# Row sums and value halves of an attention kernel, moved from VectorE and ScalarE to DMAs and TensorE

## The reference

```python
h = group_norm1(x, n1_g, n1_b)
f = dwconv(h, w3, b3) + dwconv(h, w5, b5) + dwconv(h, w7, b7)
g = sigmoid(conv1x1(f, gate_w, gate_b))
x = x + conv1x1(f * g, proj_w, proj_b)
h = group_norm1(x, n2_g, n2_b)
q, k, v = conv1x1(h, ...)             # N = 9216 pixels, 64 channels each
attn = softmax(q^T k / 8, axis=-1)    # 9216 x 9216 for each image
out = x + (attn v)^T
```

## Time and profile before

| | us |
|---|---|
| Median of 3 runs (3044.29 to 3048.2) | 3047.66 |
| The profiled execution, its own time | 3046.7 |
| Its span, first to last instruction | 3045.0 |
| TensorE busy | 2736.0 (90%) |
| GpSimd busy | 2311.9 (76%) |
| ScalarE busy | 2218.4 (73%) |
| VectorE busy | 1967.6 (65%) |
| DMAs of GpSimd's queue: 320.90 MB | 51.8% of 16 engines |

### The profile page before, as it was taken

One profiled execution on the slowest core, in us unless ns is written; L12 is line 12 of the kernel. 1 busy time (PEld: TensorE's weight loads), 2 busy tenths in 40 slices (PEclk: granted clock), 3 DMA queues, 4 the chain that ended last, 5 costly groups with the idle time before them and its releaser, 6 DMA issues.

```text
span 3045.0 us, 87180 instructions
## 1 busy us (share of the span) xinstructions
PE 2736.0 (90%) x36568; PEld 1138.5 (37%) x36568; DVE 1967.6 (65%) x2081; ACT 2218.4 (73%) x2288; POOL 2311.9 (76%) x2056
## 2 busy tenths in 40 slices
PE   7898999998989898999988989999999999999998
PEld 4343333333333333333333333333333333333333
DVE  4766666666666666666657666666666666666665
ACT  4577777777777777777767777777777777777777
POOL 1467777777778787877865878787888888887886
PEclk9999999999999999999999999999999999999999
DMA  6148666666666666666601656666666666666561
GB/s 195 35 102 182 130 131 128 129 126 129 132 127 131 128 131 127 131 133 126 122 7 41 130 125 135 132 129 130 130 135 134 134 135 134 134 135 128 124 128 21
DMA packets 124020, 371.20 MB, mean 122 GB/s; under 512 B 17640, under 2 KB 43752, under 8 KB 123120
## 3 DMA queue, kind: packets, MB, share of 16 engines
q0 software_dynamic: 88128, 320.90, 51.8%
q1 hardware_dynamic: 35504, 44.75, 5.5%
HBM read 16.41 MB, written 9.44 MB: 8 GB/s over the span
## 4 chain that ended last, share of the span: by engine, by line
PE 36%; POOL 21%; issue 13%; DVE 11%; DMA 11%; ACT 6%; POOLq 0%; ACTq 0%; SPq 0%; DVEq 0%
POOL arena L486 17%; PE ps L1060 16%; PE ps L1049 12%; DMA accD<-arena 11%; DVE mxp L827 6%; PE ps L1069 5%; ACT arena L576 3%; POOL accD L501 2%; DVE arena L853 2%; POOL mseed L519 2%; ACT ps L617 2%; PE ps L1182 2%; DVE accD L850 1%; ACT pvx L591 1%; DVE pvc L874 1%
## 5 line engine op out<-in xcount | busy, mean ns | idle before, releaser
L827 DVE TENSOR_REDUCE mxp<-ps 128x1 f32<-128x1024 f32 x1296 | 1581.0, 1224 | 775.2 <-PE ps L1069 774.1
L486 POOL TENSOR_TENSOR arena<-arena 128x512 f32<-128x512 f32 x1224 | 1703.2, 1391 | 417.7 <-ACT arena L576 351.9
L576 ACT ACTIVATE arena<-ps,bnd 128x1024 f32<-128x1024 f32 x1296 | 1382.0, 1110 | 502.3 <-PE ps L1049 483.8
L1060 PE MATMUL ps<-arena,vals 64*64 64x512 f32 x10368 | 1294.6, 613 | 0.2 <-DVE pvc L874 0.2
L1049 PE MATMUL ps<-arena 64*64 64x512 f16 x15552 | 1087.0, 382 | 145.1 <-ACT ps L617 140.1
L617 ACT ACTIVATE ps<-mseed 128x1024 f32<-128x1024 f32 x612 | 628.8, 1027 | 176.6 <-POOL mseed L519 125.5
L1049 PEld LDWEIGHTS ps<-arena 64*64 64x64 f16 x15552 | 463.1, 108 | 589.8 <-issue 322.1
L1069 PE MATMUL ps<-arena,QM 64*64 64x512 f16 x5184 | 528.5, 395 | 121.8 <-DVE mxp L827 116.9
L501 POOL DMA_DIRECT2D accD<-arena x544 | 494.4, 910 | 94.2 <-DMA accD<-arena 56.4
L1060 PEld LDWEIGHTS ps<-arena,vals 64*64 64x64 f32 x10368 | 385.0, 137 | 419.9 <-issue 333.7
L1069 PEld LDWEIGHTS ps<-arena,QM 64*64 64x64 f16 x5184 | 153.5, 105 | 664.1 <-DVE mxp L827 574.3
(11 more groups left out here) (124 smaller groups left out, 807.1 us busy)
## 6 DMA issues: line engine op xcount, KB each, us to landing
accD<-arena POOLq DMA_DIRECT2D x612, 512.0 KB, 5.1
arena<-arena SPq DMA_DIRECT2D x144, 64.0 KB, 3.5
arena<-in_x_rows SPq DMA_DIRECT2D x8, 816.0 KB, 9.7
xs<-in_x SPq DMA_DIRECT2D x4, 1152.0 KB, 15.5
f_scratch<-arena SPq DMA_DIRECT2D x32, 144.0 KB
f<-f_scratch SPq DMA_DIRECT2D x16, 288.0 KB, 9.7
QM<-arena SPq DMA_DIRECT2D x72, 64.0 KB, 3.5
xst<-arena SPq DMA_DIRECT2D x72, 64.0 KB, 4.4
```

The costliest lines, as they stand in the source:

```text
L486: nc.gpsimd.tensor_tensor(accA[:, n % 2, :], accA[:, n % 2, :], e, ALU.add).then_inc(adda_free, 1)
L576: nc.scalar.activation(E[:, :, slot_of(n % 2, p), :], ps[:, S_BANK + 2 * buf:S_BANK + 2 * buf + 2, :], ACT.Exp, scale=bnd[:, 6:7]).then_in ...
L827: nc.vector.reduce_max(flat(mxp[:])[:, v:v + 1], flat(ps[:, bank:bank + 2, :]), AX.X).then_inc(mx_free, 1)
L1060: a = nc.tensor.matmul(ps[C * t:C * t + C, ACC_BANK + r, :], V[rows, p, t, :], E[rows, t, slot_of(par, p), :], start=(p == 0), stop=(p == ...
```

## The change

It alters five things at once.

- **Fills from the fp16 row.** `fill_source`, `mseed` and its semaphore go. `seed` reads the fp16 row in `QS` itself, waits for `m_ready`, and ScalarE does the scaling in the same instruction.
- **Dumps at an even pace.** `accD` has a second copy for alternate blocks, so the first dump of a block is issued after pair 1 and then one after every odd pair, 18 in all as before.
- **Folds as DMAs.** `sum_dumps` on VectorE goes, and so does `total` on GpSimd but for an image's last block. In the next block GpSimd issues three accumulating DMAs: after pair 5 one that adds the one half of `accD` to the other (512 KB), after pairs 8 and 11 one each that adds 512 columns of it to `accA` (256 KB), each waiting for the one before. TensorE sums `accA` directly, after pair 18 and not 12.
- **Value halves by TensorE.** `turn_pv` and `sum_pv` go. `twice` is a 128 x 64 matrix with two identities; `value_sums` multiplies `pvc` by it right behind the row sums, two matmuls of 256 columns into the same PSUM bank. ScalarE copies 512 columns instead of 256 to `fin`.
- **Order on the engines.** VectorE does `add_pv` behind the first `reduce_max` of a block and not ahead of it; the reciprocals follow after the visits of pairs 17 to 24, one each, and before only after odd ones; the multiplication on GpSimd is after pair 31, not 33. Between the images the same steps move by a few chunks.

```diff
-ROW_SUMS = 12
+ROW_SUMS = 18
-DUMP_AFTER = (8, 9, 11, 12, 14, 15, 17, 18, 20, 21, 23, 25, 27, 29, 31, 33, 35, 35)
-DUMPS_SUMMED = 6
+NDUMP = NPAIR // 2
+FOLD_AFTER = (5, 8, 11)
...
+            def fold_dumps(b, j, i):
+
+                n, d = blk(b, j), dumped_block(b, j)
+                if i == 0:
+                    for k in (0, 1):
+                        pool.wait_ge(dumped[k], dumps_before(b, j + 1, 0))
+                    pool.dma_start(accD[:, d % 2, 0, :], accD[:, d % 2, 1, :], accum_op=ALU.add).then_inc(folded, 16)
+                else:
+                    pool.wait_ge(folded, folds_before(d, i))
+                    pool.wait_ge(adda_free, NSLOT + NPAIR * (n + 1))
+                    pool.dma_start(accA[:, n % 2, :], accD[:, d % 2, 0, (i - 1) * CH:i * CH], accum_op=ALU.add
+                                   ).then_inc(folded, 16)
...
             def attend(b, j):
                 n = blk(b, j)
-                fill_source(n)
                 first_a(n)
...
+                for p in range(1, NPAIR):
+                    if p > 1:
+                        add_a(n, p)
+                    if j < LASTS and p % 2:
+                        dump(b, j, p // 2)
+                    if j and p in FOLD_AFTER:
+                        fold_dumps(b, j - 1, FOLD_AFTER.index(p))
+                    if j and p == 31:
+                        normalize(n - 1)
...
-                act.wait_ge(mseed_ready, n + 1)
+                act.wait_ge(m_ready, n + 1)
                 act.wait_ge(e_ready, NPAIR * n + p)
-                nc.scalar.activation(ps[:, S_BANK + 2:S_BANK + 4, :], mseed[:, n % 2, :].unsqueeze(1).to_broadcast([P, 2, CH]), ACT.Copy
-                                     ).then_inc(seeded, 1)
+                nc.scalar.activation(ps[:, S_BANK + 2:S_BANK + 4, :], QS[:, n % 2, 2, :].unsqueeze(1).to_broadcast([P, 2, CH]), ACT.Copy,
+                                     scale=ONE * C).then_inc(seeded, 1)
...
+            def value_sums(n, bank):
+                pe.wait_ge(acc_free, n + 1)
+                for h in (0, 1):
+                    a = nc.tensor.matmul(ps[C * h:C * h + C, bank, HCH:CH], twice[:], pvc[:, h, :], start=True, stop=True)
                 a.then_inc(rs_ready, 1)
 
-            def row_sums(n, bank):
-                pe.wait_ge(sum_ready, n + 1)
+            def row_sums(b, j, bank):
+                n = blk(b, j)
+                if j < LASTS:
+                    pe.wait_ge(folded, folds_before(dumped_block(b, j) + 1, 0))
+                    sums = accA[:, n % 2, :]
+                else:
+                    pe.wait_ge(sum_ready, b + 1)
+                    sums = accS[:]
```

More of the change, by code:

```diff
@@ L555, in _ @@
                 if b + 1 < B:
-                    total(blk(b, NBLK - 1))
+                    total(b)
         @block.scalar
@@ L583, in move_pv @@
                 if n:
-                    act.wait_ge(pv_summed, 2 * n)
+                    act.wait_ge(rs_ready, n)
                 nc.scalar.activation(flat(pvc[:]), ps[:, ACC_BANK, :], ACT.Copy).then_inc(acc_copied, 1)
[L587 to L591, removed]
             def copy_row_sums(n, bank):
@@ L675, in _ @@
                         move_pv(blk(b, 0) - 1)
-                    if b and c == 4:
-                        turn_pv(blk(b, 0) - 1)
-                    if b and c == 3:
+                    if b and c == 6:
                         copy_row_sums(blk(b, 0) - 1, MX_BANK + 1)
@@ L843, in add_b, with sums_out @@
                     nc.vector.tensor_tensor(ps[:, SUM_BANK, :], ps[:, SUM_BANK, :], e, ALU.add).then_inc(addb_free, 1)
[L845 to L855, removed]
+            def sums_out(b):
                 dve.wait_ge(addb_free, NPAIR * (b + 1))
-                if n:
-                    dve.wait_ge(sum_ready, n)
+                if b:
+                    dve.wait_ge(sum_ready, b)
                 nc.vector.tensor_copy(accB[:], ps[:, SUM_BANK, :]).then_inc(accb_out, 1)
-                dve.wait_ge(accb_out, n + 1)
+                dve.wait_ge(accb_out, b + 1)
             def reciprocals(n, k):
@@ L911, in attend @@
                         reduce_max(NVIS * (n + 2) + v, v)
+                    if j and p == 0:
+                        add_pv(n - 1)
                     if j == LASTS and p + 1 < NPAIR:
                         add_b(b, n, p + 1)
[L914 to L917, removed]
                     if j == 0 and p < NPAIR - AHEAD and p % 8 == 7:
@@ L932, in _ @@
             row_masks()
+            nc.vector.tensor_tensor(twice[:], ident[:, 0:C], ident[:, C:P], ALU.add).then_inc(twice_ready, 1)
             row_stats(0)
@@ L963, in _ @@
                         add_pv(blk(b, 0) - 1)
-                    if b and c in (4, 5):
-                        for k in range(RECS // 2 * (c - 4), RECS // 2 * (c - 3)):
+                    if b and c in (6, 7):
+                        for k in range(RECS // 2 * (c - 6), RECS // 2 * (c - 5)):
                             reciprocals(blk(b, 0) - 1, k)
-                    if b and c == 6:
-                        sum_pv(blk(b, 0) - 1)
+                    if b and c == 8:
                         normalize(blk(b, 0) - 1)
-                    if b and c == 7:
-                        write_out(b - 1, NBLK - 1)
                 x1_stats(NCH - 1)
+                if b:
+                    write_out(b - 1, NBLK - 1)
                 dve.wait_ge(bn_done, NCH * (b + 1))
@@ L1013, in _ @@
             add_pv(n)
-            sum_pv(n)
             dve.wait_ge(rs_ready, n + 1)
@@ L1198, in _ @@
             pe.wait_ge(conv_out, BESIDE)
+            pe.wait_ge(twice_ready, 1)
             pe.wait_ge(mat_in, 32)
```

114 lines of the change are left out of this document (53 added, 61 removed).

## The result

The changed kernel takes 2754.76 us (median of 4 runs, 2749.4 to 2756.6) against 3047.93 us before: ratio 0.9035, 95% interval 0.9019 to 0.9052. The profiled execution took 2755.12 us, 291.6 us less than the one before.

The account below looks back on a forecast made before the run. TensorE was taken as the bound mid-block, late GpSimd fills at the edge. 78.5 - 7.7 (gaps) - 2.4 (clock) + 1.1 (added) = 69.5 us a block; 288 us less over 32 blocks plus 12 gave 2747 us, range 2690 to 2840.

Parts of the forecast that it names:

- Step 1 and 2, fills and clock: At the block's edge on TensorE: the 4.03 us gap for fills goes, and 2.4 us of low clock with it.
- Step 3, add_pv: At the block's edge: the 0.79 us gap for a maximum goes, but weigh waits 0.5 us for add_pv.
- Step 4, sum_dumps: On TensorE: the 1.82 us gap a block for a maximum behind sum_dumps' two additions on VectorE goes.
- turn_pv and sum_pv: On TensorE: gaps of 0.77 and 0.27 us a block go when these two steps leave ScalarE and VectorE.
- Step 5, value sums: On TensorE behind the row sums: two fp32 matmuls add 0.6 us a block to the path.
- A block: The period of one block falls from 78.5 to 69.5 us, for 32 blocks 288 us less.
- GpSimd: GpSimd's block: 65.0 us of work, 1.4 fold wait, 1.0 dump waits, together 67.4 us, 2 us under TensorE.
- The last blocks: The last block of each image has the same edge without dumps or maxima: 6.1 us less each, twice is 12.
- the fold's wait: On GpSimd: the fold after pair 8 waits for its DMA by 1 to 2 us.
- B: Rival: GpSimd and its DMAs become the bound, 72.0 us a block, 2827 us in all; chance 0.19.
- C: Rival: the edge keeps a 2.5 us gap and the clock falls, 73.9 us a block, 2896 us; chance 0.08.
- D: Rival: slower, GpSimd stands while each fold lands; at 14 us a fold, 3160 us; chance 0.03.

Follow-up runs that it names:

- the fills alone: Kernel before the change, with only ScalarE's fills taken from the fp16 row and fill_source gone: 2855.95 us, ratio 0.9363 against the kernel before.

## Why the prediction came out as it did

Forecast 2747, measured 2754.76 us. By its steps:

- **Step 1 and 2, fills and clock**: 4.03 + 2.4 us an edge. The mechanism is shown by the fills alone: 194 / 34 = 5.7 us an edge, of which 3.2 are waits and 2.6 clock. The wait was read from one edge longer than the average; the prediction's check, that the waits of the trace make 7.6 us a block and the edge shown 7.68, holds for the sum only, since that edge has more of the waits for fills (4.80 us for 140.1 / 34 = 4.1) and less of those for maxima (2.88 for 3.4). What the prediction did not see is that the dumps' pace works on the same gap: with the pace changed, the old fills would have cost 32 us and not 200. The sum came out right because it counted the gap once.
- **Step 3, add_pv**: 0.5 us forecast, taken between two bounds, and 0.52 + 0.19 = 0.71 in the edge shown, for another cause: that these are near each other is luck. The wait for add_pv is 0.19 us, 6.6 in all for the 17 that the prediction named as a sign; the 0.52 is a `write_out` of 1.59 us where one that lies alone takes 0.47, and with GpSimd held back it goes. The prediction had no term for an instruction that takes longer beside another engine's.
- **Step 4, sum_dumps**: forecast 1.82 us a block, 51 / 34 = 1.5 measured. **turn_pv and sum_pv**: 0.77 + 0.27 forecast, less 0.6 for the matmuls, so 0.4 net; measured from the changed kernel's side 74 / 34 = 2.2. As a measure of that the term was mis-sized, in sum_pv: in the changed kernel GpSimd is adding just when VectorE adds the halves, which take 1154 ns each in the mean for 615 in the kernel before. What undoing this part costs is thus not what the change gained by it; the gain against the kernel before was not measured by itself.
- **Step 5, value sums**: 0.6 forecast, 0.53 measured.
- **A block**: 69.5 forecast, 69.56 measured. The agreement to 0.1 us is partly luck: the waits for fills gave less than forecast, the clock more, and the mean holds one block of 83.7 us that nobody forecast.
- **GpSimd**: its sum of 67.4 us left 2 us; the slack was 3.9. The fold in whole landed after 7.1 us, as worked out, and GpSimd waited 47.3 / 34 = 1.4 us for landed folds (7.5 of the 47.3 once, beside the loads). What was too high is mostly the work: GpSimd is busy for 62.98 us in the window of a block, for 65.0 forecast, though the earlier trace rows had 63.26 and the prediction itself says that the work stays the same. The waits at the head of a block are 0.35 us in the edge shown, for 1.0. All first folds, issue to landing, and all accumulating dumps:

```profile
DMA to landing us min/median/max: 4.5/7.1/23.1
```

```profile
DMA to landing us min/median/max: 4.4/5.0/20.9
```

- **The last blocks** were put at 12 us. The 32 blocks gave 286.0 of a forecast 288, all the rest together 5.6 of 12: this term carries most of the miss of 8 us. It was taken from one edge, 6.1 us for each image. The traces show 2.6 us less from the last block of the first image to the second block of the other (217.16 us for 219.71 between GpSimd's first adds) and 4.1 less from the second image's last block to the end (68.61 for 72.73), and 0.8 us more before block 1. What holds the time there was not tested.
- **Signs.** The clock over the edges (1.00), the waits for fills (7.3 us, under 20), the block and the fold's wait came as named. Two did not: the waits for maxima are 32.5 us and not under 30, because of `write_out`, and those for add_pv 6.6 and not 17.
- **Rivals.** B fell: ScalarE waited 10.6 us in all for dumps, and 5.2 us of added work cost 1.3. C fell: no gap over 1.2 us at a usual edge. D fell: the slowest first fold of all other blocks took 8.7 us; beside the loads one took 23.1, and there TensorE did wait for it, once.

By an estimate from the figures of the Trainium skill, DMA: Bandwidth & Descriptors (Anatomy of one DMA), which the prediction weighed, a DMA of 512 KB would take 3.2 us; the dumps' median is 5.0 and that of the first folds 7.1, so the row was the better guide, and the wait at the second fold is real (1.84 us behind the edge shown).

## What to carry to other kernels

When a stall has a chain of two causes (here a helper in an engine's line, and that engine's lateness), undoing either can take most of it, so test the pair together before giving a part its share. Ask of each small instruction not only how long it takes in the trace, but what the engine beside it does at that moment, since a reordering elsewhere can triple it, as it did with `write_out` here. And read slack by adding work: the forecast sum of work and waits left 2 us where adding gave 3.9.

## What the runs showed of the hardware that I had not expected

A VectorE instruction with two operands in SBUF takes 0.47 us alone and 1.59 us when a GpSimd add of 1.26 us starts with it, while the add keeps its 1.26 us; held apart it is 0.47 again. In the kernel before, every `write_out` that no GpSimd add or multiplication overlapped took 0.47 to 0.48 us. Two additions of 64 x 256 took between 0.40 and 2.33 us each, by the rows for the same reason: the pairs that lay beside no GpSimd instruction took 0.85 to 0.87 us together. That pair was not held apart. The Trainium skill, SBUF — State Buffer (Who interferes with whom), says that a VectorE instruction with two SBUF inputs contends with a GpSimd instruction that reads SBUF; the traces agree. By that rule the maxima, read from PSUM, are untouched, and their mean is 1224 ns in both kernels.
